# A macaron block on one core: transposes on the whole array, projection and V at the end of PE's step

## The reference

```python
x = x + 0.5 * ffn(layernorm(x))
x = x + attn(layernorm(x))          # attn adds its own input and ends in a norm with gamma and beta
x = x + 0.5 * ffn(layernorm(x))

def ffn(x):                         # w_gate, w_up: [352, 128], w_down: [128, 352]
    h = silu(fp4_linear(x, w_gate)) * fp4_linear(x, w_up)
    return fp4_linear(h, w_down)    # fp4_linear rounds both operands, in blocks of 16, to an FP4 grid

def attn(x):                        # 16 heads of 64
    p = softmax(q @ k.T / 8); o = p @ v
    y = o @ w_proj + b_proj + x
    return norm(y) * ln_gamma + ln_beta
```

## Time and profile before

| | |
|---|---|
| Median of 3 runs | 2568.18 us (2564.86 to 2571.95) |
| Profiled execution | 2570.78 us, of which the span is 2569.0 us |
| Mean granted TensorE clock | 0.963 |
| PE busy | 2312.5 us, 90% |
| DVE busy | 1721.6 us, 67% |
| POOL busy | 1412.9 us, 55% |
| ACT busy | 1202.1 us, 47% |

### The profile page before, as it was taken

The page is one execution under the profiler, slowest core; times in us unless marked ns, Lnnn a source line. Parts: engine busy times, 40 slices in busy tenths (PEclk is TensorE's granted clock), DMA queues, the critical chain, the costliest instruction groups (busy, mean ns, idle before and its releaser), DMA issues.

```text
span 2569.0 us, 45690 instructions
## 1 busy us (share of the span) xinstructions
PE 2312.5 (90%) x16292; PEld 1220.1 (47%) x16292; DVE 1721.6 (67%) x2830; ACT 1202.1 (47%) x1813; POOL 1412.9 (55%) x1323
## 2 busy tenths in 40 slices
PE   3799899999999999999989998999999999999984
PEld 1344444545454454545444454454545455454542
DVE  4465677767677776767667676776767677765643
ACT  1345454545545454544545444454454545444431
POOL 2255555656556565556556555565655656555551
PEclk7799999999999999999999999999999999999985
DMA  1000000000000000000000000000000000000000
GB/s 49 5 6 2 3 5 6 6 2 10 3 6 6 2 10 2 10 2 6 6 3 10 2 10 3 6 6 2 10 3 6 6 2 10 2 6 2 6 2 9
DMA packets 167394, 16.40 MB, mean 6 GB/s; under 512 B 148160, under 2 KB 166784, under 8 KB 167168
## 3 DMA queue, kind: packets, MB, share of 16 engines
q1 hardware_dynamic: 167168, 13.39, 4.5%
HBM read 7.03 MB, written 4.19 MB: 4 GB/s over the span
## 4 chain that ended last, share of the span: by engine, by line
PE 67%; DVE 20%; issue 6%; ACT 6%; POOL 1%; DVEq 0%; DMA 0%; SPq 0%; ACTq 0%; POOLq 0%
PE pS L943 16%; PE pO L970 12%; PE pM L927 8%; DVE nmax L779 7%; PE pX L991 5%; PE pM L1085 5%; PE pX L955 4%; PE pM L980 3%; PE FpF L284 2%; PE LpF L284 2%; PE FpF L295 2%; PE LpF L256 2%; PE LpF L267 1%; DVE QL L901 1%; PE FpF L256 1%
## 5 line engine op out<-in xcount | busy, mean ns | idle before, releaser
L646 POOL TENSOR_TENSOR ES<-ES,E 128x512 f32<-128x512 f32 x512 | 693.4, 1375 | 265.1 <-ACT E L731 263.5
L779 DVE TENSOR_REDUCE nmax<-pX 128x2 fp32r<-128x1024 f32 x512 | 622.1, 1215 | 161.2 <-PE pX L955 158.3
L731 ACT ACTIVATE E<-pS 128x1024 f32<-128x1024 f32 x512 | 523.2, 1022 | 420.4 <-PE pS L943 408.7
L970 PE MATMUL pO<-E,VA 128*64 128x512 f32 x2048 | 554.6, 620 | 0.0
L640 POOL TENSOR_TENSOR ES<-E 128x512 f32<-128x512 f32 x256 | 320.5, 1274 | 366.0 <-ACT E L731 366.0
L943 PE MATMUL pS<-QH,KH 64*128 64x512 f32 x1024 | 258.7, 501 | 19.6 <-issue 15.1
L927 PE MATMUL pM<-xf,w_raw 128*64 128x512 f32 x1024 | 268.1, 600 | 3.1 <-DVE QL L901 2.4
L741 ACT ACTIVATE KH<-pM 128x512 fp32r<-128x512 f32 x128 | 76.6, 598 | 358.2 <-PE pM L927 358.2
L955 PE MATMUL pX<-KH,QH 64*128 64x512 f32 x1024 | 233.2, 405 | 4.2 <-DVE nmax L779 2.7
L943 PEld LDWEIGHTS pS<-QH,KH 64*128 64x128 f32 x1024 | 96.8, 185 | 285.2 <-issue 253.8
L991 PE MATMUL pX<-wp,ON 128*64 128x128 f32 x2048 | 141.6, 280 | 98.9 <-DVE nmax L779 79.3
(11 more groups left out here) (141 smaller groups left out, 3402.0 us busy)
## 6 DMA issues: line engine op xcount, KB each, us to landing
RROW<-RC SPq DMA_DIRECT2D x512, 2.0 KB, 2.0
xin<-in_L_attn_x SPq DMA_DIRECT2D x16, 256.0 KB, 2.8
SH<-nmax SPq DMA_DIRECT2D x256, 2.0 KB, 2.0
LC<-LROW SPq DMA_DIRECT2D x256, 2.0 KB, 2.1
out<-X SPq DMA_DIRECT2D x16, 256.0 KB, 2.3
w_raw<-in_L_attn_w_q SPq DMA_DIRECT2D x1, 512.0 KB, 4.0
w_raw<-in_L_attn_w_k SPq DMA_DIRECT2D x1, 512.0 KB, 5.6
w_raw<-in_L_attn_w_v SPq DMA_DIRECT2D x1, 512.0 KB, 6.7
```

The source lines that it names most:

```text
L646: ins = g.tensor_tensor(ES[par][:, hd, :], ES[par][:, hd, :], E[s][:, hd, :], ALU.add)
L731: a.activation(E[s][:, :, :], pS[:, :, :], ACT.Exp).then_inc(s_exp, 1)
L779: v.tensor_reduce(nmax[px % 2][:, :, t:t + 1], pX[:, :, :], AX.X, ALU.max, negate=True).then_inc(s_max, 1)
L970: ins = pe_.matmul(pO[half(hd), :], VA[of][:, kt, j * 128 + 64 * hd:j * 128 + 64 * hd + 64], E[kt][:, hd, :], start=kt == 0, stop=kt == KT ...
```

## The change

It has three parts. Turns use PE's transpose instruction: one for a block of 128, on all 128 rows and columns of the array. h's third block becomes its last 128 columns (224 to 351), so that columns 224 to 255 come twice; w_down is loaded so that the third block of its transpose has zeros in the 32 rows that belong to them, by two DMAs in place of one. The down projection then uses all 128 rows in each block. Second, in PE's stream `project` (s = 1) and the V round (s = 3) move behind the FFNs' matmuls of the same step, `project` also behind `per_head(1)`. Third, in DVE's stream the Yacc addition moves behind QL and KL, still before the FFNs' other operations.

```diff
     def pe_turn(self, dst, src):
-        for n in range(2):
-            ins = self.nc.tensor.matmul(dst[half(n), :], src[:, 64 * n:64 * n + 64], self.ident[:, :], start=True, stop=True)
-        return ins
+        return self.nc.tensor.transpose(dst, src, self.ident[:, :])
...
         for ch in range(FT):
-            for n in range(2):
-                f0 = ch * 128 + 64 * n
-                w = min(64, FF - f0)
-                ins = self.nc.tensor.matmul(self.pF[64 * n:64 * n + w, ch * 128:(ch + 1) * 128], row[:, f0:f0 + w],
-                                            self.ident[:, :], start=True, stop=True)
+            f0 = min(ch * 128, FF - 128)
+            ins = self.nc.tensor.transpose(self.pF[:, ch * 128:(ch + 1) * 128], row[:, f0:f0 + 128], self.ident[:, :])
...
-                rows = min(128, FF - ch * 128)
                 for n in range(2):
                     ins = self.nc.tensor.matmul(self.pF[half(n), t * D:(t + 1) * D],
-                                                self.hqT[0:rows, ch, t * 128 + 64 * n:t * 128 + 64 * n + 64],
-                                                self.wdT[0:rows, ch, :], start=ch == 0, stop=ch == FT - 1)
+                                                self.hqT[:, ch, t * 128 + 64 * n:t * 128 + 64 * n + 64],
+                                                self.wdT[:, ch, :], start=ch == 0, stop=ch == FT - 1)
...
-                sp.dma_start(wraw[:, 2, 0:FF], w_down).then_inc(s_wraw, 16)
+                sp.dma_start(wraw[:, 2, 0:256], w_down[:, 0:256]).then_inc(s_wraw, 16)
+                sp.dma_start(wraw[:, 2, 256 + FP - FF:FP], w_down[:, 256:FF]).then_inc(s_wraw, 16)
...
-                dve.wait_ge(s_wraw, 80)
+                dve.wait_ge(s_wraw, 96)
...
-                        if s == 1 and there(i - 3, NP):
-                            bo, yp = (b, bpar) if p >= 3 else (b - 1, 1 - bpar)
-                            dve.wait_ge(s_proj, i - 2)
-                            dve.wait_ge(s_y0, bo + 1)
-                            wait(dve, s_yacc, i - 3)
-                            v.tensor_tensor(Yacc[yp][:, :], pX[:, 0, :], Yacc[yp][:, :], ALU.add).then_inc(s_yacc, 1)
                         if s == 0 and there(i + 2, NP):
...
+                        if s == 1 and there(i - 3, NP):
+                            bo, yp = (b, bpar) if p >= 3 else (b - 1, 1 - bpar)
+                            dve.wait_ge(s_proj, i - 2)
+                            dve.wait_ge(s_y0, bo + 1)
+                            wait(dve, s_yacc, i - 3)
+                            v.tensor_tensor(Yacc[yp][:, :], pX[:, 0, :], Yacc[yp][:, :], ALU.add).then_inc(s_yacc, 1)
                         first_ffn(b, t, bpar)
                         last_ffn(b, t, bpar)
...
-                        if s == 1 and there(i - 3, NP):
-                            project(i, p)
                         if s == 1 and there(i + 2, NP):
                             pe.wait_ge(s_qlo, i + 3)
                             per_head(1, p2, x).then_inc(s_k, 1)
                         if s == 2 and there(i - 1, NP):
                             row_sums(i - 1, 1 - p % 2)
+                        first_ffn(b, 4 * p + s, bpar)
+                        last_ffn(b, 4 * p + s, bpar)
+                        if s == 1 and there(i - 3, NP):
+                            project(i, p)
                         if s == 3:
...
                                 ins.then_inc(s_v, 1)
-                        first_ffn(b, 4 * p + s, bpar)
-                        last_ffn(b, 4 * p + s, bpar)
```

## The result

The changed kernel takes 2404.6 us (median of 4; 2403.5 to 2406.4) against 2566.5 for the kernel before (2560.9 to 2572.0). The ratio is 0.937, with a 95% interval of 0.9348 to 0.9392. The forecast was 2438 us in a range of 2395 to 2510. So the time saved is 162 us where 131 were forecast.

A forecast was written before the change was run, and what follows sets the result against it. PE was taken as the bound, with waits for DVE. Savings of 93 + 7 + 29 + 13 = 142 us, less 8%, gave 131; 2570.8 became 2440, and 2438 us as median, range 2395 to 2510.

The forecast's parts named there:

- What bounds it: PE, by its waits for nmax: PE busy 90% of the span; the projection's 98.9 us of idle, with eight waits for nmax per batch, 6.5 us.
- Projection last, 93 us: Projection behind K's and the FFN's matmuls, which cover its wait for nmax: 6.1 us saved per batch, 93 us in all.
- brackets: Listed waits of PE, here the projection's for nmax; a waited start was priced at its bracket plus 0.24 us.
- V costs and saves little: V round last in its step: step 7's wait and restart go, 7 us; ACT's later VA costed at nothing.
- The new wait, Yacc: The next step's maxima wait for Yacc to read pX: 0.2 us late at t = 17, 0.3 with the restart.
- Transposes, 29 us: Turns of h and x as whole-array transposes at 0.107 us a block: 1.8 us saved per batch, 29 us.
- The 32-column tile: Last two records of an old turn of h, 32 columns wide; changes of column tiling cost up to 0.34 us.
- Start and end, 13 us: Exposed turns at both ends of the run: 9.6, 2.6 and 1.9 us saved, 0.5 lost to w_down's second load.
- 8% off for DVE's pace: PE's savings return nothing where DVE is the pace, 11.7 of 149.8 us: 142 us become 131.
- DVE's share of the chain: Named sign: DVE's part of the chain that ended last, a fifth before the change, would grow.
- The rival that DVE takes the pace: Yacc and the FFN's operations come late in several steps, half of the 142 us goes: 2497 us; 15 in 100.
- The slower rival, the clock: Turns send PE's clock to its low level; one step each would give over 3200 us; 6 in 100.

The follow-up runs named there:

- order-only run: Kernel before with the projection, V round and Yacc addition moved as in the change, turns as before: 2485.7 us, ratio 0.9662 to the kernel before.
- statistics behind ON: Changed kernel with DVE's statistics of the norm of y moved behind ON and nmax, their root on POOL a step later: 2363.9 us, ratio 0.9189 to the kernel before.
- Yacc ahead of KL: Changed kernel with the Yacc addition back in DVE's old place in front of KL: 2427.7 us, ratio 0.9437 to the kernel before.
- turns only: Kernel before with whole-array transposes and the padded w_down, PE's and DVE's order as before: 2521.1 us, ratio 0.9791 to the kernel before.

## Why the prediction was right, and where it was off

- **What bounds it: PE, by its waits for nmax.** Right. The projection's idle time fell by 72 us and the batch by 9.7.
- **Projection last, 93 us, and V, 7.** Right in mechanism, and somewhat too large. The order as a whole gave 79 us in the steady part and 89 in all, where 100 less the 8% taken off for DVE is 92. The projection's move alone gave 75 us, where 93 less 8% is 86. By steps, the brackets left in the changed kernel are 0.30, 0.61, 0.67 and 0.18 at steps 5, 21, 25 and 13. The prediction had 0.31 at step 5 and 0.65 at step 25; at step 21 it had 0.07 and at 13 none. With the old turns, in the order-only run, step 21's is 0.31. So PE, which comes there earlier with each saving in front of it, waits longer for an nmax that comes no sooner; that is how these brackets read, no run tests it. Working from the old brackets left it out.
- **V costs and saves little.** Right: nothing measurable alone, at most some 7 us behind the moved projection, and step 11 kept its wait.
- **The new wait, Yacc.** Right in place (step 18 alone); 0.46 us for the 0.3 priced. That Yacc should stand behind KL is shown by the run with it in front, 24 us slower.
- **Transposes, 29 us.** The mechanism was right and the size wrong. This is the term that carries the miss: 64 us in the steady part beside the new order. Two of its parts were off. Entering the full array was put at 0.25 us and is 0.10. And the old turn at an odd step was put at 0.98 us in the new order (1.08 less the change to the scores' tiles), and it measures 1.09 there. The rest was nearly right. At 0.107 a transpose, leaving the array is 0.16 towards the scores (0.48 less three transposes), where 0.20 was taken, and 0.21 towards 64 columns (0.05 more), where 0.25 was. The spacings of 0.09 to 0.11 bear out the 0.107. The Trainium skill's "TensorE: Matmul & The Clock Gate" (Part 4) has 275 ns, for bf16; here that is the duration of a record (0.27) and not the spacing, as the prediction took it. The 32-column tile, found in the records' gaps, is 0.35 a turn, as read.
- **The same sum with the measured pieces.** A turn of h saves 0.50 at each of four even steps (priced 0.31) and 0.45 at four odd ones (1.08 less the sum of 0.10, 0.48 and 0.05; priced 0.16, at three), xn and xm 0.29 each (priced 0.09), the turn at step 0 0.18 (priced a loss of 0.08): 4.6 us a batch for 1.8, 68 us in 15 batches. The projection's waits take 7 of it back (idle 20.1 us in the order-only run, 27.0 with the turns). That leaves 61 of the 64; the clock's shortfall, 21 us in the order-only run and 14 in the changed one, can give the rest.
- **Start and end, 13 us.** The whole change saved 24 us outside the steady part by the profiled spans (167.1 - 142.7), of which the order alone 7 (86.3 - 79.1). The turns' share is thus some 17 us, near the 13: 8 before the first turn of xm and 9 behind the last.
- **8% off for DVE's pace.** The order and the turns are worth more together (162 us) than apart (143), so DVE's pace mattered most where the old order left it in front of PE. Its 8% can't be checked as a single number. One sign that was named did not come: DVE's share of the chain was to grow, and it fell from 20% to 19%. The rival that DVE takes the pace did not come true for this change.
- **Luck.** The projection's term was some 11 us too large and the turns' 30 to 40 us too small, so part of the miss cancelled. The time came out 10 us above the range's lower end; with the projection at its full price it would have fallen just below it.
- **The slower rival, the clock.** Not by transposes: the clock's shortfall in the steady part is 14 us, less than the 21 of before and of the order-only run, which has the old turns. But the low clock does take part, after long waits. "TensorE: Matmul & The Clock Gate" (Part 4) of the Trainium skill has transposes not count as work for the clock. No run here shows whether that is so, as none has more turns than these. Between 150 us and the last turn of xm every dip, in every trace, stands behind a stop of PE of 1.75 us or more, and none behind a turn alone.

What stays open: how much of the 19 us between the sum of the halves and the whole (37 in the steady parts) is the clock and how much the waits. The turns add 29 us of idle time and 14 of shortfall in the old order, and 7 of idle time in the new, where the shortfall falls by 7. These sums are about the size of the gap, but they overlap. The stop once in two batches, at the start of step 0, stays without an explanation.

## What to carry to other kernels

A matmul that must wait for another engine's read belongs behind all work of its step that doesn't need it, and the work in front need only be as long as the wait: here the projection's move gave 75 us, and with the 0.86 us of K's matmuls alone as cover all but 12 of what the changed kernel has. Look for odd tile widths in a stream of matmuls; one last block of 32 columns cost 0.35 us, as much as six full records, and an overlapping block of full width is cheaper. When a wait is gone, ask what stands in front of the next one on the engine that sets the pace: moving 2.8 us of statistics behind the operation that PE waited for gave another 40 us.

## What the runs showed of the hardware

- A float32 transpose of 128x128 is one record, and one follows another every 0.09 to 0.11 us; an ordinary float32 matmul of the same shape is two records at 0.12 each, or four at 0.053 in halves of 64.
- Changes of tiling differ: 64 columns to the full array 0.10 us; from there to the scores' tiles 0.16 and to 64 columns 0.21, if a transpose is 0.107; a 32-column tile at the end of a turn 0.35 beyond the change that was there anyway.
- Stops of PE of 1.75 to 2.96 us, the waits at steps 5 and 11 and the stop at the start of step 0 (2.1 to 4.0 us), were at times followed by some 3 us at 1.2 GHz, in which a V round took 1.91 us instead of 0.96 to 1.01. The same stops in other batches were not: in the changed kernel 6 of 13 waits of 2.4 us at step 11 were. The shortfall of the clock was 6 us where a steady batch has no wait for another engine over 0.7 us, and only the stop at step 0 is left (statistics behind ON), 14 with a wait of 2.4 (changed), 21 with 1.8 and 2.1 (before), 31 with 3.0 (Yacc ahead of KL) and 35 with 1.8 and 2.6 (turns only). The longest wait does not set it alone: the order-only kernel has 21 us with the same single wait of 2.4 as the changed one.
